# Mirror transposes three at a time through their own PSUM bank, column transposes in turn through two banks, and the column sum copied to SBUF

## The reference, cut to what matters

```python
# x: (2048, 512) f32, adj: (2048, 2048) f32
A   = (adj + adj.T) * 0.5
A   = A + eye
deg = sum(A, axis=1)
dinv = deg ** -0.5                 # 0 where deg is not positive
adj_n = dinv[:, None] * A * dinv[None, :]
y   = (adj @ adj_n) @ x            # adj is also the coefficient matrix
out = layernorm(x + y)             # over the 512 columns, eps 1e-5
```

## Time and profile before

| | |
|---|---|
| median of 3 runs | 406.44 us |
| the profiled execution | 406.92 us, span of its instructions 405.1 us |
| busy over the span | PE 391.6 us, DVE 245.4, ACT 112.5, POOL 61.0 |
| granted TensorE clock | 0.998 of full |

### The profile page before, as it was taken

The page is one execution under the profiler, slowest core; times in us unless marked ns, Lnnn a source line. Parts: engine busy times, 40 slices in busy tenths (PEclk is TensorE's granted clock), DMA queues, the critical chain, the costliest instruction groups (busy, mean ns, idle before and its releaser), DMA issues.

```text
span 405.1 us, 5532 instructions
## 1 busy us (share of the span) xinstructions
PE 391.6 (97%) x1878; PEld 325.5 (80%) x1878; DVE 245.4 (61%) x477; ACT 112.5 (28%) x195; POOL 61.0 (15%) x95
## 2 busy tenths in 40 slices
PE   6989999999999999999999999999999999999994
PEld 5877787878888888888888888888888888888883
DVE  1887888865532622223663357777777778877742
ACT  1245455423332521112222212222222222221200
POOL 3455765732000000000000000000000000000000
PEclk9999999999999999999999999999999999999999
DMA  7999565431026762262322355555655666555300
GB/s 254 342 347 319 155 218 184 136 97 30 0 55 154 170 141 53 52 155 53 104 53 52 93 145 135 147 143 142 155 135 150 155 155 153 145 137 144 95 26 26
DMA packets 67889, 54.76 MB, mean 135 GB/s; under 512 B 3616, under 2 KB 56864, under 8 KB 67872
## 3 DMA queue, kind: packets, MB, share of 16 engines
q1 hardware_dynamic: 67872, 54.54, 50.5%
HBM read 41.94 MB, written 4.19 MB: 114 GB/s over the span
## 4 chain that ended last, share of the span: by engine, by line
issue 72%; PE 18%; DVE 4%; DMA 2%; POOL 2%; SPq 1%; ACT 0%; POOLq 0%; DVEq 0%; ACTq 0%
PE ps L424 4%; PE ps L426 4%; PE ps L425 4%; PE ps L447 3%; PE ps L455 2%; DMA lots_s<-adj 2%; POOL rstd L415 1%; DVE store L687 1%; DVE lots_s L687 1%; DVE c L716 1%; DVE col_acc L711 0%; DVE u_lo L746 0%; PE ps L468 0%; PE ps L436 0%; DVE c_lo L721 0%
## 5 line engine op out<-in xcount | busy, mean ns | idle before, releaser
L670 ACT ACTIVATE w_hi<-store 128x512 fp32r<-128x512 f32 x64 | 39.8, 631 | 122.9 <-DVE store L822 122.9
L424 PE MATMUL ps<-u_hi,w_hi 128*128 128x512 f32 x176 | 69.6, 395 | 0.0
L425 PE MATMUL ps<-u_lo,w_hi 128*128 128x512 f32 x176 | 68.5, 389 | 0.0
L426 PE MATMUL ps<-u_hi,store_lo 128*128 128x512 f32 x176 | 68.5, 389 | 0.0
L822 DVE STREAM_TRANSPOSE store<-store 128x512 f32<-128x512 f32 x64 | 65.5, 1071 | 0.0
L761 DVE SCALAR_TENSOR_TENSOR z_raw<-ps,dinv_half,z_raw 128x512 fp32r<-128x512 f32 x16 | 11.9, 751 | 73.2 <-ACT z_raw L625 73.2
L415 POOL TENSOR_TENSOR rstd<-var_eps,mhalf 128x1 f32<-128x1 f32 x16 | 8.8, 549 | 287.3 <-DVE var_eps L872 287.3
L424 PE MATMUL ps<-z,w_hi 128*128 128x512 f32 x128 | 49.8, 389 | 0.0
L425 PE MATMUL ps<-z,w_hi 128*128 128x512 f32 x128 | 49.8, 389 | 0.0
L426 PE MATMUL ps<-z,store_lo 128*128 128x512 f32 x128 | 49.8, 389 | 0.0
L424 PE MATMUL ps<-store_lo,w_hi 128*128 128x512 f32 x128 | 49.8, 389 | 0.0
(11 more groups left out here) (87 smaller groups left out, 566.5 us busy)
## 6 DMA issues: line engine op xcount, KB each, us to landing
store<-adj SPq DMA_DIRECT2D x65, 256.0 KB, 4.4
u_x<-x SPq DMA_DIRECT2D x16, 256.0 KB, 4.3
z<-z_raw SPq DMA_DIRECT2D x32, 128.0 KB, 2.3
store_lo<-z_raw SPq DMA_DIRECT2D x32, 128.0 KB, 2.3
x_res<-x SPq DMA_DIRECT2D x16, 256.0 KB, 2.6
out<-y_out SPq DMA_DIRECT2D x16, 256.0 KB, 2.0
lots_s<-adj SPq DMA_DIRECT2D x13, 256.0 KB, 4.0
col_slot<-adj SPq DMA_DIRECT2D x6, 448.0 KB, 8.4
```

Of the source, the lines that this page charges most:

```text
L424: nc.tensor.matmul(out_, hi, mov_hi, start=first, stop=False)
L425: nc.tensor.matmul(out_, hi, mov_lo, start=False, stop=False)
L426: return nc.tensor.matmul(out_, lo, mov_hi, start=False, stop=last)
L670: nc.scalar.activation(w_hi2(j)[:, CB * g:CB * g + CB], turned[j][:, CB * g:CB * g + CB], ACT.Copy).then_inc(s_hi2, 1)
```

## The change

- The banks: mirrors go in groups of 3 blocks (`CB - 1`) through the first 384 columns of bank `G + 1`, whose last 128 columns hold the column sums; column chunks use `tp[0]` and `tp[1]` in turn for all steps below 12, so a chunk waits only for the add of the chunk before the last.
- Mirror groups of row k are cut from the end of the row by threes: 5, 5, 4, 4, 4, 3, 3, 3, 2, 2, 2 groups for rows 1 to 11, 37 in all, in place of 4, 4, 4, 3, 3, 3, 3, 2, 2, 2, 1, 31 in all. The first two groups read the lot (one did before).
- The column sum's matmul moves from behind the first unit of the step to just before the second mirror group. It shares the mirrors' bank, so PE starts it when ACT has stored the first group, starts the third group only when ACT has also copied the sum, and the next row's first group too.
- ACT copies each column sum to SBUF (`store_sums`, 15 new instructions), between the second and third mirror copy; DVE's `degrees` reads the copy.
- On DVE, `u_low(k-1)` now comes behind chunk 0 and `lot_low(k-1)` behind chunk 1, in steps 2 to 11. `lot_low` waits for two mirror groups.

```diff
@@
-        csum = ps[:, G + 1]
+        csum = ps[:, G + 1, (CB - 1) * P:]
         tp = [ps[:, n].rearrange("p (b c) -> p b c", c=P) for n in (G + 2, G + 3)]
+        tm = ps[:, G + 1].rearrange("p (b c) -> p b c", c=P)
@@
         def mirrors_of(k):
-            parts = [(i, max(b0, k + 1), b1) for i, (b0, b1) in enumerate(chunks_of(k)) if b1 > k + 1]
-            return parts[-1:] + parts[:-1]
+            ends = [(max(b - CB + 1, k + 1), b) for b in range(NB, k + 1, 1 - CB)]
+            return [(next(i for i, (c0, c1) in enumerate(chunks_of(k)) if c0 < b1 <= c1), b0, b1) for b0, b1 in ends]
+
+        def lot_mirrored(k):
+            return mirror_at(k) + sum(b1 > NR for _, _, b1 in mirrors_of(k))
@@
         def bank_of(k, i):
-            return i % 2 if k < 2 else 0
+            return (chunk_at(k) + i) % 2 if k < NR else 0
@@
             def transpose_cols(k, i, b0, b1):
-                pe.wait_ge(s_add, chunk_at(k) + i - (k == 1 and i > 0))
+                pe.wait_ge(s_add, chunk_at(k) + i - (k < NR))
@@
-            def mirror(k, n, i, b0, b1):
+            def mirror(k, n, i, b0, b1, with_sums):
                 pe.wait_ge(s_add, chunk_at(k) + i + 1)
                 if n:
                     pe.wait_ge(s_mir, n)
+                if with_sums:
+                    col_sums(k + 1)
+                else:
+                    pe.wait_ge(s_csr, k + (n > mirror_at(k)))
                 for b in range(b0, b1):
-                    last = nc.tensor.transpose(tp[1][:, b - b0], row(k, b, b + 1)[:, 0], ident[:])
+                    last = nc.tensor.transpose(tm[:, b - b0], row(k, b, b + 1)[:, 0], ident[:])
                 last.then_inc(s_tm, 1)
@@
             def col_sums(k):
                 pe.wait_ge(s_near, k)
-                pe.wait_ge(s_deg, k)
+                pe.wait_ge(s_csr, k - 1)
@@
-                first = k <= NR
+                first = k == 1
@@
-                        mirror(k - 1, n, i, b0, b1)
+                        mirror(k - 1, n, i, b0, b1, n == mirror_at(k - 1) + 1)
@@
+            def store_sums(k):
+                act.wait_ge(s_ones, k)
+                nc.scalar.activation(csum_s[:, k:k + 1], csum[:, k:k + 1], ACT.Copy).then_inc(s_csr, 1)
@@
-                    store_mirrors(k - 1, 1, NC)
+                    store_mirrors(k - 1, 1, 2)
+                if k >= 1:
+                    store_sums(k)
+                if 1 <= k - 1 < NR:
+                    store_mirrors(k - 1, 2, NB)
@@
-                    dve.wait_ge(s_ones, k)
-                    nc.vector.tensor_scalar(deg[:, k:k + 1], csum[:, k:k + 1], row_sum[:, k:k + 1], 0.5, ALU.add,
+                    dve.wait_ge(s_csr, k)
+                    nc.vector.tensor_scalar(deg[:, k:k + 1], csum_s[:, k:k + 1], row_sum[:, k:k + 1], 0.5, ALU.add,
@@
                 if 1 <= k < NR:
-                    dve.wait_ge(s_tm, mirror_at(k) + 1)
+                    dve.wait_ge(s_tm, lot_mirrored(k))
@@
                     if 2 <= k < NR and i == 0:
+                        u_low(k - 1)
+                    if 2 <= k < NR and i == 1:
                         lot_low(k - 1)
-                    if 2 <= k < NR and i == 1:
-                        u_low(k - 1)
```

More of the change, by code:

```diff
@@ L126, in build @@
         part_sum = sb("part_sum", [P, NB, 5], F32)
+        csum_s = sb("csum_s", [P, NB], F32)
         row_sum = sb("row_sum", [P, NB], F32)
@@ L142, in build @@
         idle = ps[:, G + 1, 0:P]
-        csum = ps[:, G + 1]
+        csum = ps[:, G + 1, (CB - 1) * P:]
         tp = [ps[:, n].rearrange("p (b c) -> p b c", c=P) for n in (G + 2, G + 3)]
+        tm = ps[:, G + 1].rearrange("p (b c) -> p b c", c=P)
         parked = [ps[:, m].rearrange("p (b c) -> p b c", c=P) for m in range(G)]
-        acc_rest = [ps[:, G + 3], csum, ps[:, G + 2], ps[:, 0]]
+        acc_rest = [ps[:, G + 3], ps[:, G + 1], ps[:, G + 2], ps[:, 0]]
         acc2 = [ps[:, 1], ps[:, 2]]
@@ L168, in build @@
         s_ones = sem("col_sum_in_psum")
+        s_csr = sem("col_sum_stored")
         s_rsum = sem("row_summed")
@@ L584, in store_mirrors @@
                     act.wait_ge(s_tm, mirror_at(k) + n + 1)
-                    nc.scalar.activation(store[:, b0:b1, k - 1], tp[1][:, 0:b1 - b0], ACT.Copy).then_inc(s_mir, 1)
+                    nc.scalar.activation(store[:, b0:b1, k - 1], tm[:, 0:b1 - b0], ACT.Copy).then_inc(s_mir, 1)
+            def store_sums(k):
+                act.wait_ge(s_ones, k)
+                nc.scalar.activation(csum_s[:, k:k + 1], csum[:, k:k + 1], ACT.Copy).then_inc(s_csr, 1)
             def corner_high(k):
```

## The result

The changed kernel takes 413.98 us in the median (413.68 to 414.15, 4 runs), the kernel before 406.78 in the runs beside it: ratio 1.0175, 95% interval 1.0162 to 1.0187. That is 7.2 us slower. The profiled execution's span is 412.2 us for 405.1.

A forecast was written before the change was run, and what follows sets the result against it. PE, busy 61.00 of 64.10 us from 22 to 86.1, was to follow the slackless POOL-ACT-DVE loop; row 11's first unit 7.8 us late, other terms hidden or zero: 406.44 + 7.8 = 414.2 us, 8 in 10 within 408.5 to 418.

The forecast's parts named there:

- The loop as the bound: Steps 2 to 11: POOL's accumulation, `dinv`, ACT's `u_high`, DVE's `u_low`, POOL again; 6.05 us a round, no slack.
- What comes back: POOL's `dinv` shrinks while DVE stands idle: up to 0.46 us back in steps 4 to 7, some 0.3 in the last.
- 10.35 gross: Add of chunk 1 and `lot_low` moved into the loop: 0.84 to 1.24 us a step, 10.35 us up to step 10.
- the lower bound: More of POOL's rows shrink: nine rounds by 0.24 and four by 0.45, 4 us off the delay, low end 410.2.
- PE follows the loop: PE's steps 5, 8, 10, 12 late; first unit of row 11 7.8 us late, then no gap to the end.
- m2: Step 5's third mirror group on PE, forecast to start at 49.1, behind ACT's `u_high(4)` and copies.
- Which PE time is lost: PE idle 7 to 10 us more between 22 and 95, before mirrors and first units, none before column chunks.
- Mirrors by threes: Six more ACT copies cost some 0.8 us, no term; 1.4 us in steps 2 and 3 beside the loop, not added.
- a ring: Mirror groups of 3 through one bank, PE to ACT's copy and back: 1.1 us a round.
- rival B: Only the mirror ring counts, POOL's rounds shortening as much as they lengthen: 407.8 us; chance 0.07 for 407.3 to 409.5.
- Columns through two banks: Removes up to 2.1 us of PE's column-bank waits, but PE then waits for mirror ring or loop: 0.
- The copy of the sum: 15 one-column ACT copies at 0.2 us, 3 us hidden except step 12; DVE's SBUF read 0 to -0.1.

The follow-up runs named there:

- the third version with the new order: Kernel before with two column banks, shared bank, copied sum and DVE's new order, but mirror groups of up to 4: 413.50 us, +6.8 on the kernel before.

## Why the prediction was right

- **The number**: 414.2 was forecast and 413.98 measured, but the difference was 7.8 for 7.2; the kernel before ran 0.34 us above the median that the forecast starts from, and that this closes most of the gap is luck.
- **The loop as the bound** of the changed kernel was right, and the runs show it as a cause: DVE's order alone makes +7.6, and with PE's bank wait away 0, 3.8 and 6.8 us follow the length of what stands between `u_low` and POOL. For the kernel before "it has no slack" is shown one way only: a longer loop is paid, but half a microsecond of POOL's work taken out of each round won 0.4 to 0.8 us in all. Nine starts were forecast within 0.25 us, the ninth with the largest error.
- **What comes back**: the rounds grew by 6.1 us up to row 9 for 10.35 gross. `dinv` fell to 0.19 in every round, as put, and the power of the last round to 0.55 from 1.07, where some 0.3 had been put for that round. The next-column step stayed at 0.70 and the diagonals at 0.46 to 0.90, so the lower bound's further relief didn't come.
- **PE follows the loop**: step 5 was to have m2 at 49.1 and end at 51.8; it was 48.73 and 51.62. The first unit of row 11 was 7.1 us late for 7.8: `u_low(10)` started 0.5 earlier than I had it (85.78 for 86.3), and from the degree of row 12 to that unit it took 2.44 us for the 2.67 of before. The copy of step 12's sum does stand on the path, as forecast: DVE waits 0.43 us for it.
- **Which PE time is lost** was mis-sized: 7 to 10 us of added idle were forecast, 5.0 were measured, with 2.1 more in rows that show as busy. DVE's wait for `u_high` is 13.7 us, where some 10 had been put.
- **Mirrors by threes** were costed as a ring only, 27.7 and 36.3 us for the first units after steps 2 and 3; they started at 27.76 and 36.35. What I left out is that `lot_low` now waits for the second group. It didn't show, because `u_high` is later, but rival B's 407.8 was no price of it: with the old order the groups of three cost 5.2 us. Had DVE's order been left alone, the same working would have missed most of that.
- **Columns through two banks** were put at zero. On the old order that holds together with the shared bank and the copies (407.02), and as it was put: the waits went over to the mirrors. With the new order the second bank is worth 1.2 us, and 3 with the clock: the changed kernel would be slower without it. The term was read from the waits of the kernel before, which the other edit makes larger.
- **The copy of the sum**: 0.16 to 0.17 us for the 0.2 taken, hidden up to step 12. DVE's read of it from SBUF takes 0.21 to 0.22 us, for 0.22 from PSUM: nothing gained, where up to 0.06 was allowed.

What stays open: whether the 0.5 us between the third version with the new order and the changed kernel is anything at all, and if so, whether it is the ring or step 12; and what the second column bank, the shared bank and the copies do one by one.

## What to carry to other kernels

When four engines hand one row's values round, find the closed path first, by following one round on the timeline until the same instruction comes again: if each start is close behind its releaser's end (here within 0.2 us), an instruction moved into that path is paid once a round, less what the others on it get shorter (here 6.1 of 10.35 us were left), whatever the engines' busy shares are. An instruction moved ahead of its input on an engine that works in order takes all that is queued behind it into the wait; here that put up to 1.24 us a step into the loop, beside new banks that could win back 2.1 us of waits in all. And a wait that looks spare may keep two engines off one port: before it is taken away, look at what then runs beside what.

## What the runs showed of the hardware

- A DVE subtraction with both inputs in SBUF (128x512, 0.69 us) took 2.73, 2.45 and 2.18 us when it began some 0.45 us into a POOL addition of 2.63, 2.35 and 2.08 us, and ended 0.55 us after it. The other way round, POOL's 128x1 product takes 0.19 alone, and 0.65 beside that subtraction; its 128x1 power takes 0.55, and 0.99 beside another DVE instruction with two SBUF inputs.
- The granted TensorE clock fell from 1.00 to 0.50 (1.2 GHz) after several short stops of PE and one more of 0.72 us; it stayed at full speed in the profiled execution of the changed kernel, where that last stop was missing. Without POOL's wait, and with one column bank, it came and went between runs of one kernel: 411.99 to 415.43 us, and 415.18 to 420.12. The Trainium skill (TensorE: Matmul & The Clock Gate, Part 1) has the clock as throttled by default and released by activity, with two levels. The traces show the two levels, with passes of 0.43 and 0.23 us; what releases the clock no run here tests.
